# Self attention's inputs made one stage earlier, half of the weights loaded for cross attention, and two reorderings, in a four-layer decoder on one core

## The reference

```python
x = x + tanh(g_xattn[0]) * L0_xattn(layernorm(x), ctx, ctx)      # 16 heads, 16 wide
x = x + tanh(g_ffn[0])   * L0_ffn(layernorm(x))                   # experts by position
x = x + tanh(g_xattn[1]) * L1_xattn(layernorm(x), ctx, ctx)
x = x + tanh(g_ffn[1])   * L1_ffn(layernorm(x))                   # low-rank experts
x = x + tanh(g_xattn[2]) * L2_xattn(layernorm(x), ctx, am, pm)    # self, cross, relu
x = x + tanh(g_ffn[2])   * L2_ffn(layernorm(x))                   # product keys
x = x + tanh(g_xattn[3]) * L3_xattn(layernorm(x), ctx, ctx, mask, pad)
x = x + tanh(g_ffn[3])   * L3_ffn(layernorm(x))                   # routed experts

# L2_xattn, its first part: self attention
inv_mask = 1.0 - attention_mask * padding_mask
scores = q @ k.T / 4 + inv_mask * -1e9      # then softmax, @ v, @ wo + bo
h1 = ln(x + attn_out, g1, be1)

# L2_ffn: product keys
sim = einsum(h @ Wq, keys); top 8 of each half; top 8 of the 64 sums
w = silu(h . down_embed[idx]) * softmax(scores)
out = w . up_embed[idx] + (silu(h @ Wg + bg) * (h @ Wu + bu)) @ Wd + bd

# L3_ffn: each row goes to its best two of 8 experts
out = einsum('te,eth->th', c, y)
```

## Time and profile before

| | |
|---|---|
| median of 3 runs | 2996.66 us (2990.73 to 2996.67) |
| the profiled execution | 2993.17 us, of which the span is 2991.4 us |
| mean granted TensorE clock | 0.922 of full speed |
| busy, share of the span | PE 87%, PEld 68%, DVE 60%, ACT 44%, POOL 36% |
| DMA | 363.52 MB, mean 122 GB/s |

### The profile page before, as it was taken

How to read it: one execution, slowest core, us unless ns; L and a number is a source line. 1 busy time by engine, 2 the same in 40 slices (tenths; PEclk the granted TensorE clock), 3 DMA queues, 4 the chain that set the end, 5 groups by cost and what they waited for, 6 DMA issues and landing times. The chain is left out here.

```text
span 2991.4 us, 57049 instructions
## 1 busy us (share of the span) xinstructions
PE 2594.2 (87%) x21112; PEld 2029.1 (68%) x21112; DVE 1783.7 (60%) x3897; ACT 1314.9 (44%) x2656; POOL 1086.5 (36%) x1335
## 2 busy tenths in 40 slices
PE   8999599987997999869699898777968994899995
PEld 8999377884875666536377664544545873899994
DVE  5555687136864333258487436786667874566665
ACT  4444266314662111147466433344333662455552
POOL 3444311003111222257612222543353112677772
PEclk9999699997997999989799999888978996899997
DMA  8888765336640000053475300000008643455663
GB/s 236 237 246 241 200 169 155 117 109 185 172 143 16 1 1 0 18 163 75 125 189 158 115 0 1 1 0 1 1 28 218 178 119 120 169 201 214 214 218 107
DMA packets 153095, 363.52 MB, mean 122 GB/s; under 512 B 26496, under 2 KB 110336, under 8 KB 137136
## 3 DMA queue, kind: packets, MB, share of 16 engines
q1 hardware_dynamic: 141120, 275.13, 32.4%
q0 software_dynamic: 11760, 85.51, 8.1%
HBM read 271.43 MB, written 88.67 MB: 120 GB/s over the span
## 5 line engine op out<-in xcount | busy, mean ns | idle before, releaser
L1078 ACT ACTIVATE arena<-ps 125x448 f32<-125x448 f32 x768 | 405.2, 545 | 323.0 <-PE ps L986 319.6
L1112 DVE TENSOR_REDUCE arena<-ps 112x2 f32<-112x750 f32 x384 | 348.6, 931 | 83.1 <-PE ps L970 79.9
L468 POOL TENSOR_SCALAR ln_var<-ln_mv 112x1 f32<-112x1 f32 x144 | 35.4, 246 | 764.6 <-DVE ln_mv L462 762.2
L2750 PE MATMUL ps<-moe_x_r,moe_w_r 128*128 128x256 f32 x2016 | 255.8, 288 | 4.3 <-DVE arena L2903 2.9
L986 PEld LDWEIGHTS ps<-arena,wreg 98*125 98x125 bf16 x2304 | 214.9, 142 | 62.3 <-issue 19.4
L2750 PEld LDWEIGHTS ps<-moe_x_r,moe_w_r 128*128 128x128 f32 x2016 | 249.4, 194 | 8.0 <-DVE arena L2903 2.8
L970 PE MATMUL ps<-wreg,arena 96*112 96x375 bf16 x768 | 217.6, 372 | 29.9 <-DMA arena<-query_parts 16.6
L986 PE MATMUL ps<-arena,wreg 98*125 98x112 bf16 x2304 | 236.5, 227 | 4.9 <-ACT arena L1078 2.9
L996 PE MATMUL ps<-arena 125*17 125x112 f32 x6144 | 199.8, 263 | 0.6 <-ACT arena L1078 0.6
L2316 POOL TENSOR_TENSOR arena<-arena 112x1024 f32<-112x1024 f32 x64 | 121.0, 1904 | 198.3 <-DVE arena L2439 155.1
L395 POOL TENSOR_TENSOR arena<-arena 128x375 bf16<-128x375 f32 x128 | 113.7, 911 | 186.4 <-ACT arena L338 186.4
(11 more groups left out here) (345 smaller groups left out, 5691.3 us busy)
## 6 DMA issues: line engine op xcount, KB each, us to landing
wreg<-key_parts SPq DMA_DIRECT2D x288, 187.5 KB, 3.9
key_parts<-arena SPq DMA_DIRECT2D x128, 281.2 KB, 4.0
arena<-query_parts SPq DMA_DIRECT2D x108, 224.0 KB, 4.6
values<-arena SPq DMA_DIRECT2D x64, 357.0 KB
arena<-values SPq DMA_DIRECT2D x64, 357.0 KB
arena<-key_parts SPq DMA_DIRECT2D x96, 187.5 KB, 3.9
query_parts<-arena SPq DMA_DIRECT2D x40, 336.0 KB, 2.5
wreg<-in_e_w SPq DMA_DIRECT2D x16, 704.0 KB, 5.4
```

Of the source, the lines that this page charges most:

```text
L1078: act.activation(probs[k % PROBS], ps[0:KN, 4 + k % 2, 0:GT], ACT.Exp, scale=scale).then_inc(at_probs, 1)
L1112: dve.tensor_reduce(negmax[r % 2][:, 2 * p:2 * p + 2], ps[0:T, 2 * (p % 2):2 * (p % 2) + 2, 0:S2], AX.X, ALU.max, negate=True).then_inc(at ...
L2750: mm = pe.matmul(ps[:, f % 4, q * BS:(q + 1) * BS], w_r[wp][:, q, c, f * 128:(f + 1) * 128], x_r[u][xp][:, c, :], start=(n == 0 and c == 0 ...
```

## The change

There are five edits.

1. A cross attention's `load` brings matrices 0 and 3 alone (query and output); the query stage still loads all four.
2. A class `SelfInputs` takes over from `self_stage`: the masks' loads are issued in the query stage after group 0's stores, and the keys and queries of group 0 once these stores have landed. VectorE, not GpSimd, makes the mask, at the query stage's end, and adds the output bias there. In `self_stage` SyncE first loads keys and queries of group 1 and then the norm's rows; GpSimd's part begins with a wait for these rows.
3. The product-key stage has no `group_t`: TensorE reads `xn_t`, and waits for it only at the stage's start.
4. In the same stage TensorE makes the unit products of batches 0 and 1 and the next group's queries before the first output, and ScalarE's four query copies stand singly behind the third and fourth exponentials of batch 0 and the first two of batch 1.
5. In the last stage ScalarE multiplies each row's second result by its weight; VectorE adds the first results one by one and then a group's second results at once.

```diff
+                self.needed = slice(0, 4, 3) if kinds == 1 else slice(0, 4)
...
-                sp.dma_start(self.w, a["attn_w"][self.s]).then_inc(loaded, 16)
+                sp.dma_start(self.w[:, self.needed], a["attn_w"][self.s, :, self.needed]).then_inc(loaded, 16)
...
+            def mask(self, dve):
+                dve.wait_ge(loaded, self.masks_ready)
+                dve.tensor_tensor(self.pm, self.pm, self.am.unsqueeze(1).broadcast_to([T, B, T]), ALU.mult).then_inc(se_inv, 1)
+                dve.wait_ge(se_inv, 1)
+                dve.tensor_scalar(self.pm, self.pm, -1.0, 1.0, ALU.mult, ALU.add).then_inc(se_inv, 1)
+                dve.wait_ge(se_inv, 2)
+                dve.tensor_scalar(self.pm, self.pm, -1.0e9, None, ALU.mult).then_inc(se_inv, 1)
...
             def sync(sp):
                 q.load(sp)
-                for g in range(G):
+                q.store(sp, 0)
+                inputs.load_masks(sp)
+                q.stored(sp, 0)
+                inputs.load(sp, 0)
+                for g in range(1, G):
                     q.store(sp, g)
                 q.stored(sp, G - 1)
...
+            def vector(dve):
+                q.remainders(dve)
+                inputs.bias.whole(dve)
+                inputs.mask(dve)
...
             def sync(sp):
+                inputs.load(sp, 1)
                 norm.load(sp)
...
             def gpsimd(pool):
 
-                pool.wait_ge(loaded, masks_ready)
-                pool.tensor_tensor(pm, pm, am.unsqueeze(1).broadcast_to([T, B, T]), ALU.mult).then_inc(se_inv, 1)
...
+                pool.wait_ge(loaded, loaded_all)
...
+            COPIED = ((0, 2), (0, 3), (1, 0), (1, 1))
...
+            def rows(g):
+                return xn_t[:, :, g * GT:(g + 1) * GT]
...
                     if q == 0:
                         pe.wait_ge(pk_silu, n + 4)
-                    if q == 2 and g < G - 1:
-                        pe.wait_ge(pk_qc, (g + 2) * 4)
+                        if g < G - 1:
+                            pe.wait_ge(pk_qc, (g + 2) * 4)
...
+                    for q in range(2):
+                        units(g, q)
+                    if more:
+                        queries(g + 1)
                     for q in range(GB):
                         if q == GB - 1 and more:
                             similarities(g + 1)
-                        if q < 2 and g > 0:
-                            norm.evacuated(pe, (g - 1) * GB + 2 + q)
+                        if q >= 2:
+                            units(g, q)
                         out(g, q)
-                        if q == 1 and more:
-                            queries(g + 1)
...
-                            if q == 3 and hd == 1 and more:
-                                queries(g + 1)
+                            if (q, hd) in COPIED and more:
+                                query(g + 1, COPIED.index((q, hd)))
...
-                        if q == 1 and (not isinstance(g, int) or g < G - 1):
-                            stream(g + 1)
...
+                    act.activation(got[:, b, D:2 * D], got[:, b, D:2 * D], ACT.Copy, scale=coef[:, 1, b:b + 1]).then_inc(m_scaled, 1)
...
+                    dve.wait_ge(m_scaled, (g + 1) * GB)
+                    dve.tensor_tensor(x[:, some, :], x[:, some, :], got[:, some, D:2 * D], ALU.add).then_inc(m_added, 1)
```

More of the change, by code:

```diff
@@ L728, in build, with __init__ @@
         class Output:
-            def __init__(self, w, dest, gate, pieces=2):
+            def __init__(self, w, dest, gate, pieces=2, bias=None):
                 self.w, self.dest, self.gate = w, dest, gate
-                self.bias = Bias(dest, gate, attn_rows[0:T, 1, :], pieces=pieces)
+                self.bias = Bias(dest, gate, attn_rows[0:T, 1, :], pieces=pieces) if bias is None else bias
                 self.sums = [arena.take(128, 4, T) for _ in range(2)]
@@ L1191, in self_stage @@
             out_count[0] += 1
-            group_k = [wreg.take(SROWS, H, GT, dtype=BF16) for _ in range(2)]
-            group_q = [wreg.take(SROWS, H, GT, dtype=BF16), arena.take(SROWS, H, GT, dtype=BF16)]
-            group_t = wreg.take(128, DC, GT)
-            am = wreg.take(T, T)
-            pm = arena.take(T, B, T)
-            out = Output(w, dest, gate)
+            inputs.q.append(arena.take(SROWS, H, GT, dtype=BF16))
+            group_k, group_q, group_t, pm = inputs.k, inputs.q, inputs.rows, inputs.pm
+            out = Output(w, dest, gate, bias=inputs.bias)
             norm = RowNorm(dest, **norm)
-            masks_ready = expect(2)
+            loaded_all = loads[0]
             turned = ps[:, 5, 0:DC * T]
@@ L1395, in vector @@
                 dve.memset(ps[:, SUMS, :], 0.0).then_inc(const_made, 1)
-                out.bias.whole(dve)
                 for u in range(2):
@@ L2139, in queries @@
                         for d in range(DC):
[L2140 removed]
+                            mm = pe.matmul(ps[:, TURN_BANK + c % 2, 0:GT], wq[:, d, c * 128:(c + 1) * 128], rows(g)[:, d, :], start=(d == 0), stop=(d == DC - 1))
                         mm.then_inc(pk_q, 1)
@@ L2150, in similarities, with units @@
                         mm.then_inc(pk_sim, 1)
+                def units(g, q):
+                    n = g * GB + q
+                    bank = 6 + q % 2
+                    if q < 2 and g > 0:
+                        norm.evacuated(pe, (g - 1) * GB + 2 + q)
+                    at_least(pe, pk_added, n - 1)
+                    for f in range(FC):
+                        pe.matmul(ps[0:T, bank, 0:D], hid[:, f, q * T:(q + 1) * T], wd[:, f, :], start=(f == 0), stop=False)
                 def out(g, q):
@@ L2154, in out @@
                     bank = 6 + q % 2
-                    at_least(pe, pk_added, n - 1)
-                    for f in range(FC):
-                        pe.matmul(ps[0:T, bank, 0:D], hid[:, f, q * T:(q + 1) * T], wd[:, f, :], start=(f == 0), stop=False)
                     pe.wait_ge(pk_mixed, n + 1)
@@ L2238, in turned, with query @@
                                        ACT.Copy).then_inc(pk_turnc, 1)
-                def queries(g):
+                def query(g, c):
                     at_least(act, pk_sim, g * GB)
-                    for c in range(4):
-                        act.wait_ge(pk_q, g * 4 + c + 1)
-                        act.activation(q_t[:, c, :], ps[:, TURN_BANK + c % 2, 0:GT], ACT.Copy).then_inc(pk_qc, 1)
+                    act.wait_ge(pk_q, g * 4 + c + 1)
+                    act.activation(q_t[:, c, :], ps[:, TURN_BANK + c % 2, 0:GT], ACT.Copy).then_inc(pk_qc, 1)
                 def similarities(g):
@@ L2299, in step @@
                     turned(g * GB + GB - 1)
-                queries(0)
+                for c in range(4):
+                    query(0, c)
                 similarities(0)
@@ L2804, in scalar @@
                 over_blocks(act, step)
+                for b in range(B):
+                    fetch, before_it = fetched[b // GB]
+                    if b % GB == 0:
+                        act.wait_ge(fetch, before_it + 16)
+                    if b == 0:
+                        act.wait_ge(m_act, BLOCKS * FC)
+                    act.activation(got[:, b, D:2 * D], got[:, b, D:2 * D], ACT.Copy, scale=coef[:, 1, b:b + 1]).then_inc(m_scaled, 1)
             def vector(dve):
@@ L2957, in chain @@
             lora_experts_stage(5, dict(eps=1e-5, keep=h), weights)
-            w = query_stage(2, 2)
-            self_stage(2, w, 0.25, h, one[0:T, :], dict(eps=1e-6, gain=0, keep=h))
+            w, inputs = query_stage(2, 2, h, one[0:T, :])
+            self_stage(2, w, inputs, 0.25, h, one[0:T, :], dict(eps=1e-6, gain=0, keep=h))
             weights = ReluWeights()
```

96 lines of the change are left out of this document (48 added, 48 removed).

## The result

The changed kernel takes 2978.32 us (median of 12 runs, 2966.75 to 2987.09), the kernel before 2996.66 us in the same runs. The ratio is 0.9937 (95% interval 0.9922 to 0.9952): 18.9 us faster, 14.4 to 23.4. The forecast was 2969 us, the range 2956 to 2980. The profiled execution took 2984.9 us, slower than the median, and that of before was faster than its own.

The account below looks back on a forecast made before the run. TensorE, busy 87% of the span, was taken as the bound, with gains where it idles or runs at the lower clock. 2.6 + 1.3 + 17.7 + 3.5 = 25.1 us off the profiled 2993.17 gave 2968, set to 2969; range 2956 to 2980.

Parts of the forecast that it names:

- the clock's rival: Product-key groups: lower clock and ScalarE's waits leave three groups 1.1 us gain each, the last none: 2978 us; chance 0.2.
- Query and self stage: Self stage starts 7 us later, GpSimd's first subtraction waits for ln_gain's rows until 1322.2; net gain 1.3 us.
- the head start of the four tiles ready by then: Self stage: four ready tiles follow each other at 0.93 us instead of over 4.65 us, saving 1.85 us.
- Cross attentions: Loading two of four matrices saves 1.3 us before TensorE's start in two of four stages: 2.6 us.
- The product-key stage's start: TensorE starts at 1810.5 instead of 1816.11, its queries needing neither bias nor copy: 5.6 us gain.
- The groups: Product-key stage: products moved into TensorE's 12.3 us idle time gain 3.7 us per group, 11.1 for three, last 1.0.
- Last sums: Last stage: ScalarE scales, VectorE adds four batches at once, loads then bound; gain 3.5 us.
- The first rival: Self stage: ln_gain's rows land early, its chain starts at 1310.5 and gains 11 to 13 us: 2957 us; chance 0.15.
- The slower case: Product-key groups: each ScalarE copy waits for a full lower-clock product, 8.5 us lost per group: 3005 us; chance 0.04.

## Why the prediction was right, and where it was not

The forecast of 2969 us was 9 us under the measured 2978.3, inside the stated 2956 to 2980, with its sign and its largest part right. That it is inside is in part luck. The forecast's own range was 2962 to 2975; only the room given to the clock's rival reaches 2980, and the time lies 1.7 us under that edge. What that range leaves out adds up to 0.22 by the stated chances, not to under 0.2. Two of the four terms gave nothing or a loss. Step by step, with the table's means:

- *Query and self stage's mechanism: right to a microsecond.* Forecast on the old clock: stage at 1307, TensorE 1308, the subtraction at 1322.2, held by ln_gain's rows. Measured: 1307.2, 1308.5, 1323.0. No row shows the sum's 1.5 us to the first data and its 0.7 at the end; in the change the first of group 1's loads landed 3.1 us after its issue, for 3.2 by these terms. That the rows cost by their place in the queue is shown by the kernels with the rows first (11 us sooner) and in the middle (half of it). The masks' operations were 2.01 and 1.09 us for 2.0 and 1.1; the DMA ends the stage either way, as stated.
- *Its size: wrong by 3.3 us.* The step that fails is "What is gained is the head start of the four tiles ready by then". Three tiles were ready and do run together (2.72 us), but TensorE makes further scores only behind the turning of a tile: counted from the first subtraction, the fourth starts 4.36 us later where it was 4.65, and the fifth 6.17 where it was 5.84. So the stretch behind the subtraction is no shorter (136.5 us for 135.8, with ranges that overlap). And the subtraction is 1.3 us later, not 0.6. A gain of 1.3 became a loss of 2.0, of which the 1.3 us in front of the subtraction are clear of the spread.
- *Cross attentions: the head right, the path wrong.* The head start was 1.4 and 0.7 us, near the 1.3 forecast. The step that fails is that it was summed as the stage's gain. The stages are as long as before (233.3 for 233.5, 259.7 for 258.9), and alone the edit shows no gain (0.9999, 0.9990 to 1.0008). With stages that vary by 7 to 9 us and an interval that just reaches 2.6 us, a small gain is not excluded. Behind the head the DMA engines are full, and waits there end when stores and masks land; that this takes the head's gain back is argued, and which of them decides, from run to run, stays open. 2.6 us too much.
- *The product-key stage's start: 5.8 us as forecast (5.6), less 1.0.* The query products began at TensorE's lower level before and do so now, but stay there for 5.4 us instead of 3.3; until the similarities it is 9.5 instead of 8.5 us. This was in no term.
- *The groups: the mechanism right.* A group goes from 102.3 to 98.7 us (2014.57 to 2113.25 between two rows of similarities), 3.6 for the 3.7 forecast. The first mix's place in the group moved by 2.4 us later (2.3 forecast), the third is ready 93.0 us after the group's similarities, as before (92.8), and TensorE is there before it. What was missed: the first group gains 2.0 or 3.6 and the last 0 or 2.7, and a middle group of 98.7 us was 100.2 or 100.3 in four profiles, by whether the third output falls on the lower level (5.3 to 5.9 us instead of 3.71). 10.2 us on average in all for 12.1.
- *Last sums: 4.0 for 3.5.* The loads bound, as forecast; ScalarE's scaling took 0.43 us (1.71 for four) instead of 0.55, so the last four end with VectorE's.

The sum by these means is 16.4 us; the timed ratio says 18.9, and its interval holds both. Against the forecast's 25.1 the terms give 3.3 + 3.2 + 0.8 + 1.9 - 0.5 = 8.7 us less (3.2: 2.6 and the 0.6 by which the two stages together were longer). The miss of 9.3 us is another sum: the forecast took its 25.1 off a profiled execution that was 3.5 us under the median and gave 1 back, so 2.5 us come from the base, and 6.8 from a gain that was 18.3 us between the medians.

The first rival, rows that land early, did not happen, but its price was right: 11 us, had by moving them. The clock's rival was half there: ScalarE's copies waited once in a group and cost what the forecast counted, and the lower level took 1.0 us at the stage's start and up to 3 of its groups. The slower case (copies that wait for each product) is excluded by the rows of ScalarE: in a group one of four waits for TensorE.

## What to carry to other kernels

Where loads are moved ahead, read the DMA share of the stretch they move into, and list every wait of every engine on the queue they are now in front of: two small rows that nobody used for four batches, behind twelve loads, held a whole stage for 11 us. Do not book a shorter head as a gain of the stage before looking at the stretch after it for another full resource; here the heads were shorter by 1.4 and 0.7 us and no gain of the stages was seen. Filling an idle gap in an engine is safe only after asking whose semaphore the filler waits for.

## What the runs showed of the hardware

- What was issued later on one queue landed later, by about 1 us for each load in front of it: rows behind none, six or twelve loads released GpSimd 50.7 to 52.0 us (four profiles), 57.9 (one) and 62.7 to 63.4 (five) after the same mark. Neighbours overlap: the second of the rows in the middle landed at 57.8 us, and the first load issued behind it at 57.3.
- TensorE's level after the same idle time was not the same twice: 1.88 us before an output with 3.71 us (granted clock 1.00), 1.89 us with 5.69 (0.57). With the same edits the groups took 398.5 to 398.6 us in three profiles and 401.1 to 401.3 in five. What makes the one or the other stays open.
- The same 16 query products took 7.89 us with 3.3 us of them at the lower level, and 8.93 with 5.4. Both began at it, the first after 6.15 us of idle time, the second after 0.54 us behind short turnings.
- The whole kernel differs by chip: the kernel before had medians of 2996.7, 3004.2, 3012.2, 3006.3 and 3008.8 us, so only ratios on one chip are compared here.
